# Rows of a mixture of experts sent out in portions during the attention, into slots that keep room for every token

## What is computed

```python
xn = _layernorm(x, axis=-1)
x = x + attention(xn, W_qkv, W_o) + ffn(xn, centroids, ln_g, ln_b, w1, b1, w2, b2)

# attention: 16 heads of 8, chunks of 64 tokens, one running state S per head
k = layernorm_noaffine(k)
inter = einsum('bhde,bthe->bthd', S, q_c)
scores = where(causal, einsum('bthd,bshd->bhts', q_c, k_c), 0.0)
intra = einsum('bhts,bshd->bthd', scores, v_c)
S = S + einsum('bthd,bthe->bhde', v_c, k_c)

# ffn: each token goes to the one expert (of 8) with the largest affinity
assign = argmax(x @ centroids.T, axis=1)
xn = xhat * ln_g[e] + ln_b[e]                  # a second layer norm, then the expert's factors
h = relu(xn @ w1[e].T + b1[e])                 # 128 -> 512
y = x + h @ w2[e].T + b2[e]                    # 512 -> 128
out = alpha * y + (1 - alpha) * x              # alpha = sigmoid(affinity of the chosen expert)
```

## Time and profile before

| | us |
|---|---|
| median of 3 runs (472.26 to 475.53) | 474.2 |
| the profiled execution, its own time | 471.31 |
| its span, first to last instruction | 469.5 |
| busy: TensorE / VectorE / ScalarE / POOL | 360.6 / 287.6 / 244.0 / 251.2 |
| granted TensorE clock, mean share of full speed | 0.887 |

### The profile page before, as it was taken

The page is one execution under the profiler, slowest core; times in us unless marked ns, Lnnn a source line. Parts: engine busy times, 40 slices in busy tenths (PEclk is TensorE's granted clock), DMA queues, the critical chain, the costliest instruction groups (busy, mean ns, idle before and its releaser), DMA issues. The chain is left out here.

```text
span 469.5 us, 17240 instructions
## 1 busy us (share of the span) xinstructions
PE 360.6 (77%) x6891; PEld 303.5 (65%) x6891; DVE 287.6 (61%) x771; ACT 244.0 (52%) x647; POOL 251.2 (53%) x244
## 2 busy tenths in 40 slices
PE   7879898879988441111069999975999999999992
PEld 6557666657756220000037777765999999999992
DVE  7967978866498300000027777773788877887871
ACT  4766777557647300000116666622776667776671
POOL 4573667626231777777600000000788888888885
PEclk9999999999989755555559999997999999999998
DMA  5124354640402111111112223313555555555430
GB/s 165 42 94 139 97 158 161 189 135 25 162 4 88 54 52 57 53 52 52 52 43 74 90 73 94 94 47 92 88 70 69 76 69 68 70 71 73 54 35 0
DMA packets 55150, 37.35 MB, mean 80 GB/s; under 512 B 5352, under 2 KB 51616, under 8 KB 55072
## 3 DMA queue, kind: packets, MB, share of 16 engines
q1 hardware_dynamic: 42800, 27.72, 20.1%
q0 software_dynamic: 12272, 8.54, 13.2%
HBM read 18.72 MB, written 17.97 MB: 78 GB/s over the span
## 5 line engine op out<-in xcount | busy, mean ns | idle before, releaser
L431 POOL DMA_INDIRECT out_dram<-qx,rows x71 | 112.6, 1586 | 119.4 <-DVE qx L913 97.5
L621 ACT ACTIVATE qx<-sc,b1T 128x128 f32<-128x128 f32 x284 | 81.3, 368 | 43.2 <-PE sc L1284 37.4
L386 POOL DMA_INDIRECT slots_d<-rows,pos_i x64 | 63.0, 984 | 29.9 <-issue 19.2
L1284 PE MATMUL sc<-wide,tokens 128*128 128x128 f32 x568 | 76.1, 277 | 0.2 <-ACT wide L615 0.2
L1292 PE MATMUL bank<-tokens,qx 128*128 128x128 f32 x568 | 75.1, 275 | 0.4 <-ACT qx L621 0.4
L761 DVE TENSOR_TENSOR pr<-sc,causal 128x1536 f32<-128x1536 f32 (+1 forms) x32 | 63.7, 1989 | 16.7 <-PE sc L1136 16.4
L1284 PEld LDWEIGHTS sc<-wide,tokens 128*128 128x128 f32 x568 | 69.9, 194 | 0.5 <-ACT wide L615 0.5
L1292 PEld LDWEIGHTS bank<-tokens,qx 128*128 128x128 f32 x568 | 69.0, 192 | 0.6 <-ACT qx L621 0.6
L752 DVE TENSOR_TENSOR vp<-bank,krs 128x512 f32<-128x512 f32 x16 | 11.1, 692 | 78.7 <-remote 74.7
L899 DVE COPY tokens<-xT 128x1024 f32 x71 | 56.4, 795 | 1.7 <-issue 1.6
L1190 PE MATMUL bank<-pr,vz 128*32 128x64 f32 x2048 | 40.8, 224 | 12.8 <-issue 10.1
(11 more groups left out here) (154 smaller groups left out, 563.2 us busy)
## 6 DMA issues: line engine op xcount, KB each, us to landing
rows<-slots_d SPq DMA_DIRECT2D x71, 66.0 KB, 2.0
slots_d<-empty SPq DMA_DIRECT2D x8, 528.0 KB, 4.1
res<-in_L_attn_x_dram SPq DMA_DIRECT2D x16, 256.0 KB, 3.0
out_dram<-res SPq DMA_DIRECT2D x16, 256.0 KB, 3.3
tokens<-in_L_attn_x_dram SPq DMA_DIRECT2D x7, 512.0 KB, 4.2
w1raw<-in_L_ffn_w_dram SPq DMA_DIRECT2D x8, 256.0 KB, 3.7
w2raw<-in_L_ffn_w_dram SPq DMA_DIRECT2D x8, 256.0 KB, 4.8
out_dram<-qx,rows POOLq DMA_INDIRECT x71
```

Of the source, the lines that this page charges most:

```text
L386: pool.indirect_dma_start(slots_d, bass.IndirectOffsetOnAxis(ap=pos_i[:, t:t + 1], axis=0), rows[:, t, :], None, bounds_check=NS * P - 1, ...
L431: pool.indirect_dma_start(out_rows, bass.IndirectOffsetOnAxis(ap=xs[:, a, D + 2:D + 3].bitcast(U32), axis=0), ye[:, a, :], None, bounds_ch ...
L621: last = nc.scalar.activation(ht[:, k % 2, c * P:(c + 1) * P], SC[2 + k % 2][:, c * P:(c + 1) * P], ACT.Relu, bias=b1T[:, bass.ds(e * FC + ...
L1284: last = mm(SC[2 + k % 2][:, c * P:(c + 1) * P], ws[:, k % 3, c * P:(c + 1) * P], xsT[:, k % 2, :], start=True, stop=True)
```

## The change

**Slots.** Each expert now has room for all tokens: 72 tiles of slots (`RT`), 8 experts and one common empty tile at the end, 577 tiles in HBM. A token's row is its expert's fixed start plus its rank, so that a batch can be placed as soon as it is counted. Where an expert's tokens end inside a tile, SP writes 128 empty rows behind them once the counts are known (`fill_tails`); the nine zeroing transfers are gone. In place of reading slots one after another, SP reads them by a tile number, which VectorE works out (`place_i`) and SP loads into registers, eight at a time.

**Ranking.** After `count(b)` TensorE ranks batch `b` in three matmuls (quads 2, 4, 6 and 8), and VectorE places it in the next quad.

**Sending.** POOL sends 2 tiles in each of the quads 3 to 6, 5 in each of the quads 7 and 8, and from half 18 on 4 in each half, once that half's scores are made (`sent`). Before `values_own(n)` it waits until what was sent has landed.

**Gates.** The sigmoid of the gate, one instruction before the sending, is now taken of loaded slots, 8 at a time (`se_gates`).

```diff
+        def sent(h):
+            quads = [0, 0, 0, 2, 2, 2, 2, 5, 5]
+            done = sum(quads[n] for n in range(LATE) if h > 2 * n)
+            return min(NT, done + 4 * max(0, h - ROUTED))
...
-            def zero_slots(i):
-                rows_of = slots_d.rearrange("(p k) r -> p k r", p=P)
-                last = min(RING * (i + 1), NS)
-                sp.dma_start(rows_of[:, RING * i:last, :], empty[:, 0:last - RING * i, :]).then_inc(s("slots_zero"), 16)
+            def fill_tails():
+
+                sp.wait_ge(s("zero_ready"), 2)
+                sp.dma_start(slots_d[E * RT * P:(E * RT + 1) * P, :], empty[:, :]).then_inc(s("tails"), 16)
+                sp.wait_ge(s("tail_ready"), 1)
+                regs = [sp.alloc_register(f"tail{e}") for e in range(E)]
+                sp.load(regs, tail_i[0:1, 0:E])
+                for e in range(E):
+                    row = sp.snap(regs[e], min_val=0, max_val=((E - 1) * RT + RT - 1) * P)
+                    sp.dma_start(slots_d[bass.ds(row, P), :], empty[:, :]).then_inc(s("tails"), 16)
...
+            def load_slots(i):
+
+                last = min(RING, NS - RING * i)
+                sp.load(tiles[0:last], place_i[0:1, RING * i:RING * i + last])
+                for j in range(last):
+                    k = RING * i + j
+                    a = k % DEEP
+                    tile = sp.snap(tiles[j], min_val=0, max_val=E * RT)
+                    reach(sp, s(f"out_done{a}"), 16 * (k // DEEP))
+                    sp.dma_start(xs[:, a, :], slots_v[:, bass.ds(tile, 1), :]).then_inc(s(f"se_in{a}"), 16)
+
+            sp.wait_ge(s("eid_ready"), 1)
+            sp.wait_ge(s("tails"), 16 * (E + 1))
             for a in range(2):
                 sp.wait_ge(s(f"scattered{a}"), 16 * NT // 2)
...
                 reach(pool, s("pr_even"), min(2 * n, ROUTED))
+                for a in range(2):
+                    reach(pool, s(f"scattered{a}"), 16 * ((sent(2 * n) + 1 - a) // 2))
                 pool.tensor_copy(own_columns(0, n % 2, 0), values_of(0, 0))
...
                         ln_norm(n + 2, (4,))
+                    for t in range(sent(h), sent(h + 1)):
+                        scatter_rows(t)
                 elif n + 1 < LATE:
                     values_own(n + 1)
-            for t in range(NT):
-                scatter_rows(t)
+            for h in range(ROUTED, NH):
+
+                pool.wait_ge(s("sc_ps"), h + 1)
+                for t in range(sent(h), sent(h + 1)):
+                    scatter_rows(t)
...
+            def se_gates(i):
+
+                last = min(RING, NS - RING * i)
+                for j in range(last):
+                    k = RING * i + j
+                    act.wait_ge(s(f"se_in{k % DEEP}"), 16 * (k // DEEP + 1))
+                a = RING * i % DEEP
+                nc.scalar.activation(xs[:, a:a + last, D + 1], xs[:, a:a + last, D + 1], ACT.Sigmoid)\
+                    .then_inc(s("gates"), 1)
...
+            se_gates(0)
             for i in range(ROUNDS):
...
+                    if a == RING // 2 and i + 1 < ROUNDS:
+                        se_gates(i + 1)
...
             def experts_of_slots():
-                link(nc.vector.tensor_tensor(cnt[:, 0, :], cnt[:, 0, :], cnt[:, 1, :], ALU.add))
-                link(nc.vector.tensor_tensor(eidf, over_t(cnt[:, 0, :], NS), bcast(iotk[:, :], 2, E), ALU.is_le))
-                link(nc.vector.tensor_reduce(out=iotk[:, :], in_=eidf, axis=AX, op=ALU.add))
-                nc.vector.tensor_scalar(eid_i[:, 2:NS + 2], iotk[:, :], float(E - 1), None, ALU.min)\
+
+                link(nc.vector.tensor_scalar(cnt[:, 0, :], cnt[:, 0, :], -1.0, float(RT), ALU.mult, ALU.add))
+                link(nc.vector.tensor_tensor(eidf, over_t(cnt[:, 1, :], NS), bcast(iotk[:, :], 2, E), ALU.is_le))
+                link(nc.vector.tensor_reduce(out=place[:, 0:NS], in_=eidf, axis=AX, op=ALU.add))
+                link(nc.vector.tensor_scalar(eid_i[:, 2:NS + 2], place[:, 0:NS], float(E - 1), None, ALU.min))
+                link(nc.vector.tensor_tensor(eidf, eidf, over_t(cnt[:, 0, :], NS), ALU.mult))
+                link(nc.vector.tensor_reduce(out=place[:, 0:NS], in_=eidf, axis=AX, op=ALU.add))
+                link(nc.vector.tensor_tensor(place[:, 0:NS], place[:, 0:NS], iotk[:, :], ALU.add))
+                nc.vector.tensor_scalar(place_i[:, 0:NS], place[:, 0:NS], float(E * RT), None, ALU.min)\
                     .then_inc(s("eid_ready"), 1)
...
+            def rank_tokens(b):
+
+                n = 2 * b + 2
+                tiles = slice(b * BATCH, (b + 1) * BATCH)
+
+                pe.wait_ge(s("res_ready"), n)
+                pe.wait_ge(s("counted"), b + 1)
+                to = Y[1][:, 0:BATCH * E]
+                mm(to, notbefore[:, :], ohb[:, tiles, :].rearrange("p t e -> p (t e)"), start=True, stop=False)
```

More of the change, by code:

```diff
@@ L51, in moe_attention_kernel @@
     LATE = 9
+    RT = 72
+    assert RT >= NTOK // P + 1
     PAIR = 2
@@ L652, in _ @@
             nc.vector.memset(onesb[:, :], 1.0)
+            for e in range(E):
+                nc.vector.memset(base[:, e:e + 1], float(e * RT))
             nc.vector.memset(eid_i[:, 0:2], 0)
@@ L851, in count, with second_norm @@
                         .then_inc(s("counted"), 1)
-            def second_norm():
-                link(nc.vector.tensor_tensor(tmp_nt[:, :], rstd[:, :], rstd[:, :], ALU.mult))
-                nc.vector.tensor_tensor(tmp_nt[:, :], tmp_nt[:, :], mv[:, :, 1], ALU.mult).then_inc(s("var2_ready"), 1)
-            def second_rstd():
-                dve.wait_ge(s("std2_ready"), 1)
-                nc.vector.reciprocal(rows[:, :, D], tmp_nt2[:, :]).then_inc(s("rows_done"), 1)
+            def second_norm(b):
+                tiles = slice(b * BATCH, (b + 1) * BATCH)
+                link(nc.vector.tensor_tensor(tmp_nt[:, tiles], rstd[:, tiles], rstd[:, tiles], ALU.mult))
+                nc.vector.tensor_tensor(tmp_nt[:, tiles], tmp_nt[:, tiles], mv[:, tiles, 1], ALU.mult)\
+                    .then_inc(s("var2_ready"), 1)
@@ new lines, in second_rstd, with ranks @@
+            def second_rstd(b):
+                tiles = slice(b * BATCH, (b + 1) * BATCH)
+                dve.wait_ge(s("std2_ready"), b + 1)
+                nc.vector.reciprocal(rows[:, tiles, D], tmp_nt2[:, tiles]).then_inc(s("rows_done"), 1)
+            def ranks(b):
+                dve.wait_ge(s("rank_ps"), b + 1)
+                if b == NB - 1:
+                    link(nc.vector.tensor_scalar(cnt_i[:, :], Y[1][:, BATCH * E:BATCH * E + E], float(P - 1), None, ALU.add))
+                nc.vector.tensor_tensor(rank[:, :, :], Y[1][:, 0:BATCH * E].rearrange("p (t e) -> p t e", e=E),
+                                        ohb[:, b * BATCH:(b + 1) * BATCH, :], ALU.mult).then_inc(s("rank_sb"), 1)
@@ L862, in tiles_of_experts, with places @@
+            def places(b):
+                tiles = slice(b * BATCH, (b + 1) * BATCH)
+                dve.wait_ge(s("rank_sb"), b + 1)
+                link(nc.vector.tensor_reduce(out=top[:, tiles], in_=rank[:, :, :], axis=AX, op=ALU.add))
+                nc.vector.tensor_copy(pos_i[:, tiles], top[:, tiles]).then_inc(s("route_done"), 1)
             def tiles_of_experts():
-                dve.wait_ge(s("cnt_ps"), 1)
-                link(nc.vector.tensor_scalar(cnt_i[:, :], Y[1][:, 0:E], float(P - 1), None, ALU.add))
+                nc.vector.scalar_tensor_tensor(out=tail_i[:, :], in0=cnt_i[:, :], scalar=float(1 - P), in1=tail0_i[:, :],
+                                               op0=ALU.add, op1=ALU.add).then_inc(s("tail_ready"), 1)
+                dve.wait_ge(s("tail_ready"), 1)
@@ L946, in _ @@
                         ln_stats(n + 3, range(4))
-                    if n in (2, 4, 6):
+                    if n in (2, 4, 6, 8):
+                        second_norm(n // 2 - 1)
                         choose(n // 2 - 1)
-                    if n == 8:
-                        count(3)
-                        second_rstd()
-                    if n == 9:
+                    if n in (3, 5, 7, 9):
+                        places(n // 2 - 1)
+                    if n == LATE:
+                        tiles_of_experts()
+                    if n == LATE + 1:
                         experts_of_slots()
@@ L978, in _ @@
                         result(n - 1)
+                    if n in (2, 4, 6, 8):
+                        count(n // 2 - 1)
+                        second_rstd(n // 2 - 1)
                     if stat:
@@ L1200, in output @@
                 last.then_inc(s("out_ps"), 1)
+            def rank_tokens(b):
+                n = 2 * b + 2
+                tiles = slice(b * BATCH, (b + 1) * BATCH)
+                pe.wait_ge(s("res_ready"), n)
+                pe.wait_ge(s("counted"), b + 1)
+                to = Y[1][:, 0:BATCH * E]
+                mm(to, notbefore[:, :], ohb[:, tiles, :].rearrange("p t e -> p (t e)"), start=True, stop=False)
```

(10 more changed lines are left out.)

104 lines of the change are left out of this document (40 added, 64 removed).

## The result

| | before, us | with the change, us | ratio, 95% interval |
|---|---|---|---|
| the comparison (4 runs each) | 473.23 (469.56 to 475.53) | **448.77** (446.99 to 449.33) | 0.9487, 0.9441 to 0.9533 |
| again, third chip | 473.44 | 451.11 | 0.9511, 0.9447 to 0.9576 |
| again, fourth chip | 471.27 | 440.06 | 0.9333, 0.9258 to 0.9408 |
| again, fifth chip | 471.74 | 439.38 | 0.9339, 0.9257 to 0.9421 |

Faster by 5 to 7%, where 16% were forecast: 448.8 us against a forecast of 396 us and a range that ended at 446. On the fourth and fifth chips the time lies inside that range, with the same stall in the portions as here, so it doesn't speak for the forecast's mechanism. On the second chip the kernel before took 389.1 us (387.4 to 393.0, 7 runs); the changed one has not run there.

The account below looks back on a forecast made before the run. POOL's block of 64 scatters, during which TensorE nearly idles, was taken to cost its full length; TensorE bounds the expert stage. 471.3 - 85.7 + 4 + 2.4 + 3 = 395.0, forecast 396 us, range 386 to 446.

Parts of the forecast that it names:

- The stall goes: Attention, halves 19 to 21: portions of scatters don't stall TensorE as the block of 64 did; 85.7 us go.
- The first rival: Attention: TensorE stalls in each portion of four (2.7 us) or five (4.0), none in pairs; 435 us, chance 0.18.
- Tail: After each of 14 long portions TensorE stays slow for 8.1 us, 113 us more; 548 us, chance 0.12.
- POOL held by VectorE: Each scatter waits out a VectorE mask of 1.75 us and costs 3.0 us; 442 us, chance 0.05.
- VectorE (+4): Short ranking and placing instructions per batch and in `experts_of_slots` add 4 us, between 0 and 5.5.
- TensorE's waits for the count: Quads 2, 4, 6 and 8: next half's scores stand behind `counted`, masks start 0.6 us later; 2.4 us, bounds 0 to 12.
- Begin of the expert stage: Register loads, eight slot loads, a table load and sigmoid delay the first relu by 3 us, between 1 and 6.
- POOL in quads 3 to 8: Sending two or five tiles a quad beside POOL's attention work costs 0, at most 3 us.
- Sum: Whole kernel: 471.3 - 85.7 + 4 + 2.4 + 3 = 395.0 us; forecast 396 us.
- the forecast case: Whole kernel: portions don't stall TensorE and the scattering is hidden; 387 to 412 us, chance 0.63.

Follow-up runs that it names:

- the run of threes and pairs: Changed kernel with 3 scatters in each of halves 6 to 17 and 2 in each later half: 430.87, 431.14, 430.44 and 418.60 us.
- the run without scatters: Changed kernel with all 64 row scatters sent after the last scores, none beside the attention's halves: 466.83 us, ratio 0.992.

## Why the prediction was wrong, step by step

**The stall goes (-85.7 us): this step failed.** It took for granted that portions don't stall TensorE. They do, each with the block's own signs: bursts, gaps of the same length, "issue". By half 31 the block costs 310.7 - 221.95 = 88.8 us and the portions 63.7, so 25 us went instead of 86. (The 63.7 also hold some POOL time of the early quads, told below.) The evidence that I called the best, the dense indirect DMAs of the expert stage with TensorE at 50 of 50 us, was a true row wrongly carried over. TensorE starts 9 matmuls a us there (451 in 50) and 25 a us in the attention (174 in 6.9); starved in a portion, it starts 5 (20 in 3.7), and deep in the block 0.4 (25 in 58). Whether the expert stage is spared for that, or since its scatters stand 1.9 us apart and each behind a wait, was not tried. One reading was off too: by the earlier trace rows the products stop at 153.60 (154.11 less 0.51 of idle), 2.6 us after the first scatter, not 2.4.

**The first rival was right.** It named the place (gaps marked "issue" 2 to 3 us into each portion, halves of 9 us; measured 1.6 us in the portion shown, and 10.5 us a half in the mean) and the condition, and forecast 435 us with a band of 415 to 455. Its terms were too small: 2.7 us for a run of 4 where 45.3 / 11.5 = 3.9 were measured, 4.0 for a run of 5 where the two cost 13.0 together (half 18 is 18.4 us late, half 15 was 5.4), and 0 for a pair where one cost 0.85 in halves 18 to 29 of the run of threes and pairs. It also counted 12 fours and not 11. The sum of 40 was 63.7. It counted TensorE's own gap and left out the 0.9 us after the last scatter, the lower clock that follows, POOL's own time in quads 3 to 8, and the engines that then wait one after another. ScalarE waits 31.8 us for products from 155 to 285 us; in the run without scatters it is 8.3 us from 137 to 222:

```profile
ACT y L574 <- PE bank L1253: 31.8, 7, 6.0
```

With a chance of 0.18 it was given too little: the trace of the kernel before held one cause seen beside one effect, and the forecast needed the effect to end when only the spacing changed.

**Tail (548 us):** fell. TensorE is back at full pace 0.9 us after the last scatter of the portion shown, below the 2.6 us from which it would have decided.

**POOL held by VectorE (442 us):** fell; that its number lies near the result is chance. The scatters took 966 to 1223 ns in the changed kernel, 971 in the median, against the 3.0 us of this rival; the figure of the Trainium skill that spoke for it (page "SBUF — State Buffer", section "SBUF: two separate sides", about 3100 ns) shows in none of them.

```profile
L416 POOL DMA_INDIRECT slots_d<-rows,pos_i x64: 966/971/1223, 62.9 to 277.9; - x64
```

**VectorE (+4) and TensorE's waits for the count (+2.4):** the waits are there, and longer than priced. In the changed kernel, up to half 18, TensorE sits idle for 8.0 us before the ranking matmuls, until VectorE's totals come:

```profile
PE bank L1273 <- DVE total L900: 7.1, 3, 2.9
PE bank L1273 <- DVE total L890: 0.9, 1, 0.9
```

In the run with all scatters after the scores it is 4.8 us, twice the price. Even so half 18 starts there at 137.0 us (139.6 in the run with one run of 64), where it started at 144.0, 140.9 and 141.6 in three traces of the kernel before. So on balance the two terms and what the change wins ahead of half 18 come to a gain; what won it was not taken apart.

**Begin of the expert stage (+3, 1 to 6):** at its low end. From SP's first load to the first relu it is 302.15 - 294.44 = 7.7 us, where it was 6.5; the load of registers ahead of it (0.85 us in the forecast) is not in this difference:

```profile
294.44 4.71 SPq L332 DMA_DIRECT2D rows<-slots_d  x8
...
300.73 1.28 ACT L668 ACT_TABLE_LOAD   x1 [1.98 <-DMA rows<-slots_d]
...
302.15 1.12 ACT L657 ACTIVATE qx<-sc,b1T 128x128 f32<-128x128 f32 x4
```

**POOL in quads 3 to 8, price 0, at most 3:** wrong, a smaller step. By half 18 the changed kernel is 18.4 us behind the run without portions. Memsets at the same places, which starve nothing, put it 7.4 us behind (144.36 against 136.99), and on the chip without the stall half 18 came at 139.6 to 145.7 us. So some 7 of the 18.4 us are POOL's own time and the waits for it, an estimate across two chips; the rest is starving. In halves 18 to 29 POOL's own time costs nothing, as forecast.

**Sum.** Had the stall gone as forecast and POOL's own 7 us stayed, 446.99 - 63.7 + 7 = 390 us would have come by this estimate, within the forecast case's 387 to 412: nearly all of the error is in the one step.

## What to carry to other kernels

If an engine slows down beside another engine's block of work, cutting the block into pieces moves the cost and need not remove it: ask what within one piece is still as it was. Where TensorE issues small matmuls densely, spread POOL's indirect DMAs singly or in pairs with some 2 us between (here 0.25 to 0.43 us lost for each, against 0.8 to 1.0 in fours and 1.4 in one run). Their rows and bytes made no difference here, which speaks for fewer and fuller ones; that was not tried. An engine that also has work of its own in a stretch, as POOL in quads 3 to 8, makes others wait by its time alone: replace the transfers by a memset to tell the two costs apart. And before an experiment on a stall is believed, look at the kernel before on the same chip: of the five chips here one didn't have it at all.

## What the runs showed of the hardware

- Where the stall is, indirect DMAs on POOL in one run starve TensorE's issue in the attention: from 1.6 us (the portion shown) to 2.6 us (the block) after the first. In the portion TensorE starts 5 matmuls a us instead of 25, and full pace is back 0.9 us after the last one; deep in the block it starts 0.4 a us, and full pace comes 8.1 us after the last one. 32 rows do it like 128 (half 31 at 290.3 and 289.5 us on one chip), and 128 bytes a row like 528 (282.7 against 278.2 to 289.5). Memsets of 0.95 us on POOL and portions of four plain DMAs of the same rows don't (halves 18 to 29 in 79.9 and 80.0 us). The expert stage, with 9 matmuls a us, isn't slowed by 27 accumulating indirect DMAs in 50 us.
- It goes with the chip or its state: 471 to 473 us (medians) on four chips and 389 us on a fifth, for the same kernel. The portions' price in halves 18 to 29 goes from 35.0 to 47.7 us over four traces of the changed kernel.
- The granted clock stands at half speed in slices 15 to 21 of the kernel before, the ones in which the block has TensorE nearly idle, and falls beside the portions too: 0.88 over halves 18 to 29 of the changed kernel, 1.00 without scatters. The mean goes from 0.887 to 0.934.
